# Low parts of an MLP's inner layer: where they are subtracted, and on which engine the rows' high part is cast

## The reference

```
h = layernorm(x) * (1 + ca) + sa
x = x + ga * mixer_and_mlp(h)       # windowed attention + state-space scan, then a dense MLP
h = layernorm(x) * (1 + cb) + sb
x = x + gb * moe(h)                 # 8 experts, top 2, SwiGLU

# the dense MLP, the last step of mixer_and_mlp(y):
h = layernorm(y, ln2_g, ln2_b)
y = y + gelu(h @ mlp_W1 + mlp_b1) @ mlp_W2 + mlp_b2      # 256 -> 1024 -> 256
```

## Time and profile before

| | us |
|---|---|
| three runs | 2464.19, 2482.88, 2476.2 |
| median | 2476.2 |
| the profiled execution | 2463.03 |
| its span in the trace | 2461.3 |
| granted TensorE clock, mean | 0.925 of full speed |
| busy: TensorE / VectorE / GpSimd / ScalarE | 2101.7 / 1463.8 / 1030.2 / 948.9 |

### The profile page before, as it was taken

The page is one execution under the profiler, slowest core; times in us unless marked ns, Lnnn a source line. Parts: engine busy times, 40 slices in busy tenths (PEclk is TensorE's granted clock), DMA queues, the critical chain, the costliest instruction groups (busy, mean ns, idle before and its releaser), DMA issues. The chain is left out here.

```text
span 2461.3 us, 57658 instructions
## 1 busy us (share of the span) xinstructions
PE 2101.7 (85%) x19372; PEld 1675.0 (68%) x19373; DVE 1463.8 (59%) x3737; ACT 948.9 (39%) x1734; POOL 1030.2 (42%) x1150
## 2 busy tenths in 40 slices
PE   2888989888988889898969888888349999999996
PEld 0766777666777667777746555555238888888885
DVE  6554455545455455555448888888526666666664
ACT  1222222222222222222234555555135655656553
POOL 7112121211121111212015777878536666666664
PEclk6889899999898999998989999999669999999998
DMA  3111011111011111011123444444225544555543
GB/s 103 62 48 48 28 28 38 47 47 47 16 31 47 47 47 34 22 38 47 35 71 119 129 125 126 128 127 122 56 65 100 91 90 90 92 90 92 91 93 52
DMA packets 155281, 172.70 MB, mean 70 GB/s; under 512 B 35028, under 2 KB 136023, under 8 KB 155088
## 3 DMA queue, kind: packets, MB, share of 16 engines
q1 hardware_dynamic: 101008, 96.69, 14.6%
q0 software_dynamic: 36352, 56.78, 12.4%
q10 hardware_dynamic: 17856, 18.37, 2.1%
HBM read 109.40 MB, written 53.99 MB: 66 GB/s over the span
## 5 line engine op out<-in xcount | busy, mean ns | idle before, releaser
L1832 POOL DMA_INDIRECT out<-experts_y,experts_entry x144 | 238.6, 1657 | 188.1 <-DVE experts_y L1808 163.1
L751 ACT ACTIVATE mixer_prob<-mixer_sc 128x1024 f32<-128x1024 f32 x128 | 131.2, 1025 | 454.1 <-PE mixer_sc L131 454.1
L631 PE MATMUL mixer_sc<-w_shift,w_select 128*128 128x128 bf16 x1024 | 235.2, 230 | 74.2 <-DVE w_shift L863 72.1
L642 PE MATMUL mixer_pv<-w_V,mixer_prob 128*128 128x33 f32 x2048 | 257.4, 282 | 0.0
L642 PEld LDWEIGHTS mixer_pv<-w_V,mixer_prob 128*128 128x128 f32 x2048 | 249.3, 199 | 1.9
L129 PE MATMUL mixer_sc<-mixer_Qh,w_Kz 128*128 128x128 f16 x1024 | 234.0, 229 | 0.0
L130 PE MATMUL mixer_sc<-mixer_Ql,w_Kz 128*128 128x128 f16 x1024 | 233.8, 228 | 0.0
L131 PE MATMUL mixer_sc<-mixer_Qh,w_Kz 128*128 128x128 f16 x1024 | 233.8, 228 | 0.0
L839 DVE TENSOR_REDUCE w_mx<-mixer_sc 128x4 bf16<-128x512 f32 x256 | 165.0, 684 | 88.7 <-PE mixer_sc L616 86.5
L1773 DVE TENSOR_SCALAR experts_v<-experts_v 128x512 f32<-128x512 f32 x144 | 75.8, 526 | 215.9 <-ACT experts_v L1747 215.9
L1822 POOL DMA_INDIRECT experts_rows<-scratch_xs,experts_entry x144 | 170.9, 1187 | 59.2 <-issue 42.7
(11 more groups left out here) (315 smaller groups left out, 6581.7 us busy)
## 6 DMA issues: line engine op xcount, KB each, us to landing
mixer_x<-in_x SPq DMA_DIRECT2D x16, 512.0 KB, 4.0
w_Kz<-mixer_Kt SPq DMA_DIRECT2D x64, 128.0 KB, 2.4
scratch_xs<-scratch_mod SPq DMA_DIRECT2D x16, 512.0 KB, 10.3
mixer_hres<-mixer_h SPq DMA_DIRECT2D x16, 512.0 KB, 10.7
scratch_x<-mixer_x SPq DMA_DIRECT2D x16, 512.0 KB, 3.0
mlp_xa<-scratch_x SPq DMA_DIRECT2D x16, 512.0 KB, 4.7
mlp_stage<-in_x_w SPq DMA_DIRECT2D x16, 512.0 KB, 4.4
mlp_xb<-scratch_x SPq DMA_DIRECT2D x16, 512.0 KB
```

Source lines behind the costliest of these rows:

```text
L631: pe.matmul(out, w["select"][:, var, 4 * c + j, :], w["shift"][:, n % 2, :], start=True, stop=False)
L642: last = pe.matmul(pvO[:, i, :], prob[:, n % 2, i * P:(i + 1) * P], V[:, n, i, :], start=True, stop=True)
L751: act.activation(prob[:, n % 2, :].rearrange("p (c j) -> p c j", c=2), sc[:, 2:4, :], ACT.Exp, scale=SCALE).then_inc(exped.sem, 1)
L1832: pool.indirect_dma_start(out=out, out_offset=bass.IndirectOffsetOnAxis(ap=entry[:, s, t, 0:1].bitcast(I32), axis=0), in_=y[:, s % 2, t, : ...
```

## The change

`POOLED` becomes empty. So GpSimd subtracts no low parts of the inner layer, VectorE subtracts all eight at the place where it did four (L1404, behind `norm_x1`), `hid_lo_pool` has no producer or waiter left, and `low_done` always waits for VectorE's counter. The cast of the rows' high part moves from VectorE's `split_rows` to ScalarE as `row_highs(b - 1)`, behind `copy_rows(b - 2)` and ahead of the weight piece's casts, with the three waits that it had; VectorE's subtraction behind it waits for ScalarE's counter. GpSimd keeps `send` and `residual`.

```diff
--- before.py
+++ after.py
@@ -976,7 +976,7 @@
 ROUTE = 20
 GATE_TOP = 9.0 / (1.0 + math.exp(-1.702 * 9.0))
 HB = 4
-POOLED = (0, 1, 2, 3)
+POOLED = ()
 
 
 def mlp(nc, din, w, x_w, scratch, out, NB, keep, capacity):
@@ -1216,6 +1216,12 @@
                     act.wait_ge(xT_f.sem, xT_f.at(b, k + 1))
                     act.copy(xT[0][:, k, :], xTf[:, k, :]).then_inc(xT_hi.sem, 1)
 
+            def row_highs(a):
+                act.wait_ge(s_h2.sem, s_h2.at(a, TT))
+                act.wait_ge(row_out.sem, row_out.at(a, 0))
+                act.wait_ge(hT_mm.sem, hT_mm.at(a, 0))
+                act.copy(rows[:, :, 0, :], h2[:]).then_inc(row_hi.sem, 1)
+
             def weigh(a):
                 act.wait_ge(route.sem, route.at(a, 13))
                 act.activation(gap[:], gap[:], ACT.Tanh, scale=0.5).then_inc(gapped.sem, 1)
@@ -1249,6 +1255,8 @@
                     x_parts(b + 1)
                 if behind >= 2:
                     copy_rows(b - 2)
+                if behind >= 1:
+                    row_highs(b - 1)
                 act.wait_ge(piece_in.sem, piece_in.at(b, 32))
                 for _, area, places in piece(b):
                     act.copy(places[0], area).then_inc(piece_hi.sem, 1)
@@ -1259,6 +1267,7 @@
             store_rows(NB - 2)
             copy_rows(NB - 2)
             store_x2(NB - 1)
+            row_highs(NB - 1)
             store_rows(NB - 1)
             copy_rows(NB - 1)
             weigh(NB - 2)
@@ -1316,10 +1325,6 @@
                                              in1=shsc[:, 0, :], op0=ALU.mult, op1=ALU.add).then_inc(s_h2.sem, 1)
 
             def split_rows(a):
-                dve.wait_ge(s_h2.sem, s_h2.at(a, TT))
-                dve.wait_ge(row_out.sem, row_out.at(a, 0))
-                dve.wait_ge(hT_mm.sem, hT_mm.at(a, 0))
-                dve.tensor_copy(rows[:, :, 0, :], h2[:]).then_inc(row_hi.sem, 1)
                 dve.wait_ge(row_hi.sem, row_hi.at(a, 1))
                 dve.tensor_tensor(rows[:, :, 1, :], h2[:], rows[:, :, 0, :], ALU.subtract).then_inc(row_lo.sem, 1)
```

## The result

The changed kernel took 2513.55 us (median of four runs, 2510.67 to 2522.09), the kernel before 2470.84 us in the runs beside it (four, 2464.19 to 2482.88). The ratio is 1.0173 with an interval of 1.0122 to 1.0224: slower by 42.7 us between the medians. The profiled execution took 2513.61 us, its span is 2511.8 us; against the span of before, 2461.3 us, that is +50.5.

What follows compares the result with a forecast made beforehand. In the MLP stage VectorE's chain up to norm_x1 was taken to set the batch's period. Batches 3 to 14 (31 us), 1 and 2 (6) and the last (1) give +38; the clock's 4 makes +42 on 2476.2: 2518 us, range 2493 to 2556.

Steps and rivals of the forecast that it cites:

- the third case: MLP stage: low clock covers chunks 6 and 7 in every batch, +36 us in place of 4, 2550 us; chance 0.22.
- The chain and the ring: MLP batch: VectorE's chain to norm_x1 sets the period; gelu 4 waits for low 0 behind norm_x1, delaying chunk 6 and transposes.
- Relief of place, 2.3 us: VectorE's place, no longer beside GpSimd's subtractions, falls from 3.82 to 1.5 us: 2.3 us earlier in each of batches 3 to 14.
- Ring cost, 4.9 us: Transposes start 5.1 us behind the end of norm_x1 instead of 0.22: 4.9 us later a batch, bounds 4.4 and 5.6.
- The clock, +4 us in all: TensorE's half clock behind the stops: +4 us for batches 1 and 2 and those where it now holds; bounds -20 and +36.
- The rule of the Trainium skill: A loop with a long enough idle gap in each pass returns to the low clock every pass; here all 14 batches.
- Batches 1 and 2, +6: No place there, the inverse root is relieved by 2.0 us instead; net +2.9 us a batch, 6 us for both.
- batch 0: First batch of the MLP stage: nothing booked; one batch's 2.9 us given as its bound.
- The last batch, about +1: No norm_x1 follows; low 7 ends 6.4 us behind N (norm_x1's end elsewhere) instead of 2.5, less 2.3 to 2.8 relief.
- a forecast of 0, 0, 6, 31 and 1: Terms in us: before the stage, batch 0, batches 1 and 2, 12 batches 3 to 14 at +2.6 each, last batch.
- What costs nothing: VectorE's four more subtractions (2.7 us), ScalarE's row cast (1.06 us) and GpSimd's queue writes stay covered; slack 0.8 us.
- The fast rival: Ring does not bind, gelu 4 starts on time, stop shrinks and clock holds: -50 us, 2426 us; chance 0.06.

Runs made afterwards that it cites:

- experiment 3: Changed kernel with eight hid buffers (HB = 8) instead of four: 0.987 of the kernel before, 2440.68 us.
- experiment 4: Changed kernel, four buffers kept, VectorE subtracting chunks 0 to 3 between place and the moments, ahead of norm_x1: 1.004 of the kernel before, 2485.64 us.
- experiment 6: Changed kernel with GpSimd making four unused subtractions of the same shape per batch: 1.0419 of the kernel before, 2576.72 us.
- experiment 1: Changed kernel with POOLED = (0, 1, 2, 3) again, so only the rows' cast moves to ScalarE: 0.9992 of the kernel before.
- experiment 6's second run: Changed kernel with four unused GpSimd subtractions per batch, the fourth waiting for nothing: 1.0395 of the kernel before, 2573.26 us.
- experiment 9: Changed kernel with HB = 8 and chunk 0's low part back on GpSimd (POOLED = (0,)): 0.984 of the kernel before, 2431.87 us.
- experiment 7: Changed kernel with HB = 8, place moved behind the first outer addition and GpSimd's queue writes behind the residual: 1.0016 of the kernel before, 2477.25 us.
- experiment 8: Kernel of experiment 7 with the residual's input loads also waiting for the sixth gelu of their batch: 1.0054 of the kernel before.

## Why the prediction was right

The forecast was 2518 us, +42 on the median; measured were 2513.55 and +42.7. The wait that was to cost the time is the one that did; that the two totals agree so closely is in part luck, as the sum below shows, and the clock went as the third case has it. By its own steps:

**The chain and the ring: right.** Gelu 4 starts 0.85 us behind the start of low 0 (0.7 forecast), and from there the sequence is the one written down, with a stop of 5.39 us before chunk 6 (5.2 forecast) and one of 0.78 before the transposes (about 1). Experiments 3 and 4 show that the wait is the cause: a deeper ring takes it away, or an earlier low 0, and the loss goes (in experiment 4 three quarters of it).

**Relief of place, 2.3 us: right** where the change has it: 3.82 to 1.59. Experiment 6 gives it back and more.

**Ring cost, 4.9 us: right, and the clock comes on top of it.** Batch 1 shows the ring alone, since the clock stays at 1.00 there: the transposes stand 5.15 us behind the start of low 0 (the prediction's N), where 5.1 was worked out.

```profile
1311.87 2.70 DVE L1409 TENSOR_TENSOR mlp_hidl<-mlp_hid,mlp_hidh 128x512 f16<-128x512 f32 x4
...
1317.02 1.07 PE L1122 MATMUL mlp_pj<-w_identf,mlp_nrm 128*128 128x128 f32 x8 [0.87 <-ACT mlp_hid L1249]
```

In batches 3 to 14 they stand 6.5 to 7.7 us behind it, 7.3 in the mean. The 2.2 us more are the half clock on chunks 6 and 7.

**The clock, +4 us in all: the term that was too small.** "The half clock costs the same where it covers transposes or chunk 6" does not hold. In the 14 us from the transposes on, the clock of before is 1.00 in some batches (as at 1487.02) and 0.78 to 0.90 in the others; after, it is 1.00 in all, and the low clock lies on chunks 6 and 7 of every steady batch. The period grew by 3.19 us. Of that the ring gives 4.95 (5.15 less the 0.2 at which the transposes stood before) and the low clock on chunks 6 and 7 gives 2.2, while the relief of place takes back 2.2; what is left over, about 1.7, is what the low clock had cost before (an estimate by difference, near the 1.8 that was set as its bound). Net the clock is +0.5 a batch, and the last batch, which the forecast left out, has it too.

So the third case (the low clock on chunks 6 and 7 in every batch) came true in its condition for batches 2 to 15; its price, 2.6 us a batch on top, did not, because it takes nothing off for the old loss.

The rule of the Trainium skill quoted in the prediction (page "TensorE: Matmul & The Clock Gate", section "HAM oscillation — how this bites in real kernels") is borne out in the steady batches: the batch shown falls to 0.56 behind its stop, while in experiment 3, where the longest stop in that batch is 1.72 us, the mean clock is 0.99. It is not borne out in all 14: behind 3.51 us in batch 1 the clock stays at 1.00, behind the same 3.51 us in batch 2 it is 0.66 until the transposes. Why the two differ no run shows.

**Batches 1 and 2, +6: nearly right.** The low parts of batch 3 come 7.0 us later, and 0.8 of that is from before the stage. But batch 3's own place, already relieved, stands ahead of them; without that relief (2.3 us there, 3.80 to 1.47) and without batch 0, which took 1.6 where I had nothing, batches 1 and 2 took 6.9. The half clock in batch 2 is worth 1.4 of it (its transposes stand 6.54 us behind low 0, those of batch 1 5.15).

**The last batch, about +1: wrong, it was about +3.9.** From the start of its low parts on it is 5.7 us longer, and the relief of its place, 1.8 us (3.77 to 2.01), stands ahead of them. Its low parts and TensorE's chunk 6, after:

```profile
1771.16 2.70 DVE L1409 TENSOR_TENSOR mlp_hidl<-mlp_hid,mlp_hidh 128x512 f16<-128x512 f32 x4
...
1778.24 1.29 DVE L1409 TENSOR_TENSOR mlp_hidl<-mlp_hid,mlp_hidh 128x512 f16<-128x512 f32 x2 [0.86 <-issue]
```

```profile
1772.68 0.61 PE L129 MATMUL mlp_pj<-mlp_xTh,w_w_hi 128*128 128x512 f16 x1 [3.15 <-issue]
```

Low 7 ends 8.4 us behind the first and not 6.4, because the stop brings the low clock here too, which I had left out of this batch.

**The sum.** In the profiled pair, booked as the prediction books it: 0.8 before the stage, 1.6 in batch 0, 6.9 in batches 1 and 2, 37.2 in batches 3 to 14, 3.9 in the last, 0.1 behind: +50.5 against a forecast of 0, 0, 6, 31 and 1, and 4 for the clock, 42. Between the medians it is +42.7, since the profiled execution of before lay 7.8 us under its median and that of after on its own. So the terms are 8.5 us short of the profiled pair: 3 in batches 1 to 14, mostly the clock, 2.9 in the last batch, 2.4 in batch 0 and before the stage. That the medians hide this is luck. The forecast itself is 4.5 us high because its base, 2476.2, was the median of three runs, and four give 2470.84.

**What costs nothing: right.** The first addition waits 0.29 us for TensorE, so VectorE was there first, as forecast (slack 0.3 instead of 0.8). The row cast is free (experiment 1). The queue writes are not late; one is stretched to 1.82 us:

```profile
1500.24 1.00 POOL L1452 DMA_INDIRECT scratch_queue<-mlp_entry,mlp_slot  x1 [2.90 <-DVE mlp_ids L1380]
...
1506.61 1.82 POOL L1452 DMA_INDIRECT scratch_queue<-mlp_entry,mlp_slot  x1 [0.30 <-issue]
...
1510.00 0.95 POOL L1452 DMA_INDIRECT scratch_queue<-mlp_entry,mlp_slot  x1 [0.31 <-issue]
```

**The fast rival was over-priced.** Experiment 3 makes its condition true, and gives -28.5 us between the medians (2440.68 against 2469.13 of the kernel before beside it), not the -50 I had worked out. I had let TensorE's stop shrink by all the relief and all the clock, a period of 26.2 us; the 2.4 us more of low parts on VectorE (4.90 against the 2.49 of the earlier trace rows) bind first, at 28.1.

## What to carry to other kernels

When work moves to another engine, ask where it lands in that engine's queue and who needs its *first* piece. Here four subtractions of 0.69 us were no load for VectorE, but the first stood behind an unrelated normalisation while a ring of four buffers waited for it, and 2.3 us of relief a batch became 3.2 us of loss; one constant (the ring's depth) made the same change a gain of 1.3%. Price a stop of TensorE with the clock that the rows show behind it, the last batch included, and take off what the low clock cost there before; and price a gain only up to the next engine's own queue.

## What was not expected of the hardware

- **Which VectorE operations GpSimd stretches.** In the rows of experiment 6's second run the multiplication with two SBUF inputs (L1370) takes 1.01 us, and small casts and tensor-scalar operations 0.94 to 1.24. The addition with one input in PSUM (L1369, 0.16) and the reduction (0.22) are not touched, nor are the four statistics of the earlier trace rows beside the low parts of the earlier trace rows (1.39, beside 1.41 after). The Trainium skill, page "GPSIMD Engine Reference", section "8. Key points", names contention of GpSimd with VectorE instructions "in a 2-port perf mode or with two SBUF inputs". By that rule L1370 is caught and L1369 is not, and the trace agrees. A caught operation takes about as long as one GpSimd subtraction does (1.16 us).
- **It works in the other direction too.** A queue write of GpSimd takes 0.96 us alone, 1.82 beside VectorE's low parts in the changed kernel, and in experiment 9 one took 4.23 us, most of it beside seven of them.
- **A stall without a name.** ScalarE's 3.1 us before gelu 5 in experiment 7, 2.6 us before gelu 6 in experiment 8, and VectorE's 3.33 us before an addition in experiment 6 have no releaser that the program's waits explain.
